# LoRA experts stage: masks made group by group, most router logits in the attention stage before, low-rank products one group ahead, and the B products as three rounded passes

## What is computed

```python
probs = softmax(x @ gate_w.T)                # 8 experts
vals, idx = top_k(probs, 2);  rw = vals / sum(vals)
common_w1 = x @ w_gate.T                     # shared by all experts, 256 -> 1024
common_w3 = x @ w_up.T
d1 = (x A1_e) B1_e * 2.0                     # rank 16 for each expert e
d3 = (x A3_e) B3_e * 2.0
act = silu(common_w1 + d1) * (common_w3 + d3)
out = (weight @ act) @ w_down.T + weight-sum of ((act A2_e) B2_e) * 2.0
```

## Time and profile before

| what | value |
|---|---|
| median of 3 runs | 2966.62 us (2965.15 to 2968.17) |
| the profiled execution: its own time | 2957.48 us |
| the profiled execution: its span | 2955.8 us |
| TensorE busy in the span | 2586.5 us (88%) |
| VectorE, ScalarE, GpSimd busy | 1778.2, 1340.0, 1104.7 us |
| the stage of the change, barrier to barrier | 898.1 to 1249.3 us |

### The profile page before, as it was taken

How to read it: one execution, slowest core, us unless ns; L and a number is a source line. 1 busy time by engine, 2 the same in 40 slices (tenths; PEclk the granted TensorE clock), 3 DMA queues, 4 the chain that set the end, 5 groups by cost and what they waited for, 6 DMA issues and landing times. The chain is left out here.

```text
span 2955.8 us, 56956 instructions
## 1 busy us (share of the span) xinstructions
PE 2586.5 (88%) x21304; PEld 2070.0 (70%) x21304; DVE 1778.2 (60%) x3911; ACT 1340.0 (45%) x2695; POOL 1104.7 (37%) x1396
## 2 busy tenths in 40 slices
PE   7999699997997999869699898888868994899995
PEld 7999477884875666536467666666745873899995
DVE  5665587125864333258488546787767874566665
ACT  4444366324673111147546533444433662465553
POOL 3444311003111222237612233643452112677773
PEclk9999799997998999979889999889977996899998
DMA  8887855327650000063276300000017743455663
GB/s 229 240 243 237 236 162 152 118 88 195 172 154 17 1 0 1 18 164 77 82 188 177 123 19 1 1 1 1 1 45 198 183 116 122 167 204 218 220 219 110
DMA packets 153626, 361.69 MB, mean 122 GB/s; under 512 B 26496, under 2 KB 110336, under 8 KB 138160
## 3 DMA queue, kind: packets, MB, share of 16 engines
q1 hardware_dynamic: 141632, 273.03, 32.8%
q0 software_dynamic: 11760, 85.51, 8.1%
HBM read 269.33 MB, written 88.67 MB: 121 GB/s over the span
## 5 line engine op out<-in xcount | busy, mean ns | idle before, releaser
L1210 ACT ACTIVATE arena<-ps 125x448 f32<-125x448 f32 x768 | 405.2, 545 | 328.2 <-PE ps L1118 324.5
L1244 DVE TENSOR_REDUCE arena<-ps 112x2 f32<-112x750 f32 x384 | 348.3, 930 | 84.2 <-PE ps L1102 81.2
L499 POOL TENSOR_SCALAR ln_var<-ln_mv 112x1 f32<-112x1 f32 x160 | 43.9, 275 | 759.1 <-DVE ln_mv L493 754.8
L1118 PEld LDWEIGHTS ps<-arena,wreg 98*125 98x125 bf16 x2304 | 215.9, 143 | 62.3 <-issue 19.2
L2925 PE MATMUL ps<-moe_x_r,moe_w_r 128*128 128x256 f32 x2016 | 255.0, 288 | 4.1 <-DVE arena L3085 2.7
L2925 PEld LDWEIGHTS ps<-moe_x_r,moe_w_r 128*128 128x128 f32 x2016 | 249.1, 194 | 7.2 <-DVE arena L3085 3.4
L1102 PE MATMUL ps<-wreg,arena 96*112 96x375 bf16 x768 | 216.9, 371 | 33.5 <-DMA arena<-query_parts 24.8
L1118 PE MATMUL ps<-arena,wreg 98*125 98x112 bf16 x2304 | 237.3, 228 | 4.8 <-ACT arena L1210 2.9
L1128 PE MATMUL ps<-arena 125*17 125x112 f32 x6144 | 199.1, 263 | 0.6 <-ACT arena L1210 0.6
L425 POOL TENSOR_TENSOR arena<-arena 128x375 bf16<-128x375 f32 x128 | 114.4, 917 | 169.9 <-ACT arena L362 169.9
L282 PE MATMUL ps<-kv_ctx_r,kv_w_r 128*128 128x376 f32 x768 | 146.2, 339 | 23.1 <-DVE kv_w_r L388 14.3
(11 more groups left out here) (353 smaller groups left out, 5847.8 us busy)
## 6 DMA issues: line engine op xcount, KB each, us to landing
wreg<-key_parts SPq DMA_DIRECT2D x288, 187.5 KB, 3.9
key_parts<-arena SPq DMA_DIRECT2D x128, 281.2 KB, 4.1
arena<-query_parts SPq DMA_DIRECT2D x108, 224.0 KB, 4.6
values<-arena SPq DMA_DIRECT2D x64, 357.0 KB
arena<-values SPq DMA_DIRECT2D x64, 357.0 KB
arena<-key_parts SPq DMA_DIRECT2D x96, 187.5 KB, 4.0
query_parts<-arena SPq DMA_DIRECT2D x40, 336.0 KB, 5.6
wreg<-in_e_w SPq DMA_DIRECT2D x16, 704.0 KB, 5.2
```

The lines of the kernel that those rows point to most:

```text
L1118: mm = pe.matmul(ps[0:KN, bank, g * T:(g + 1) * T], keys[r][:, hd, c * KN:(c + 1) * KN], queries(b)[:, hd, :], start=not masked, stop=not ...
L1210: act.activation(probs[k % PROBS], ps[0:KN, 4 + k % 2, 0:GT], ACT.Exp, scale=scale).then_inc(at_probs, 1)
L1244: dve.tensor_reduce(negmax[r % 2][:, 2 * p:2 * p + 2], ps[0:T, 2 * (p % 2):2 * (p % 2) + 2, 0:S2], AX.X, ALU.max, negate=True).then_inc(at ...
```

## The change

- **Logits.** 13 of the 16 sequences' router products move into the tail of `cross_stage`, 3, 3, 4 and 3 of them between the steps of its last chain; 3 stay at the head of the stage.
- **Head.** ScalarE makes the rounded half of x and of the weights, and of B1 and B3. GpSimd makes the other halves of x and of the gate and up weights, in a first part of 256 columns and a rest of 768; VectorE makes those of B. TensorE's order is: late logits, the low-rank products of group 0, the shared products of pieces 0 and 1, then the masks of group 0 alone.
- **Masks by groups.** The masks of group g + 1 are made inside group g, half at f = 3, half at f = 7. `weight_g` and the masks have two buffers.
- **B products.** The float32 product becomes three rounded ones, for which the masked low-rank values also need a rounded and a remainder part (`low_r`): 8 masking products a group where there were 4, and a difference of masks (`change`); VectorE makes 6 of the 8 and GpSimd 2, at the start of its `step(g)`.
- **One group ahead.** The low-rank products of group g + 1 run inside group g, behind the first quarter of the down products.
- A3 is loaded early, with the others.

```diff
+                if routed is not None:
+                    pe.wait_ge(early[1], routed.ready)
+                    pe.wait_ge(at_max, (n0 + B) * PAIRS)
+                logits(range(0, 3))
                 out.turn_back(pe, last, (B - 1) % 2)
+                logits(range(3, 6))
                 out.turn(pe, last, (B - 1) % 2)
+                logits(range(6, 10))
                 out.project(pe, last, (B - 1) % 2)
+                logits(range(10, B - LOGITS_LATE))
...
+            def masked_low(eng, g, part, q):
+                for k, m in ((0, mask_g[g % 2][:, 0, :]), (1, change)):
+                    eng.tensor_tensor(low_r[part][:, q, k, :], low[part][:, q, :], m, ALU.mult).then_inc(e1_lowm, 1)
+
             def gpsimd(pool):
                 top.make_ranks(pool)
+                pool.wait_ge(e1_weights, 1)
+                pool.tensor_tensor(x_r[1], xn_t[:, :, 0:GT], x_r[0].bitcast(F32), ALU.subtract).then_inc(e1_weights, 1)
+                for q in range(2):
+                    pool.wait_ge(e1_lowc, q + 1)
+                    split_w_low(pool, q, slice(0, FIRST)).then_inc(e1_wlow, 1)
+                for q in range(2):
+                    split_w_low(pool, q, slice(FIRST, F)).then_inc(e1_wlow, 1)
                 def step(g):
-                    pool.wait_ge(e1_weights, 3 * g + 3)
+                    pool.wait_ge(e1_low_lo, LOW_LO0 + 3 * (g + 1))
+                    pool.wait_ge(e1_maskc, 4 * (g + 1))
+                    masked_low(pool, g, 1, 0)
...
+                def hidden(f, k):
+                    for q in range(2):
+                        for n, (wp, xp) in enumerate(PRODUCTS):
+                            last = n == len(PRODUCTS) - 1
+                            mm = pe.matmul(ps[:, 2 + 2 * (f % 3) + q, 0:GT], b_r[wp][:, q, f * 128:(f + 1) * 128], low_r[xp][:, q, k, :],
+                                           start=False, stop=last, skip_group_check=k == 1)
+                    mm.then_inc(e1_hid, 1)
+                lows(0)
+                pe.wait_ge(e1_weights, 2)
+                pe.wait_ge(e1_wlow, W_LOW0 + 2)
+                for f in range(2):
+                    base(f)
+                for half in range(2):
+                    masks(0, half)
...
+                            if g > 0 or f >= 2:
+                                base(f)
+                            if f == 0:
+                                pe.wait_ge(e1_lowm, (g + 1) * 8)
+                            hidden(f, 0)
                         if f > 0:
                             pe.wait_ge(e1_act, g * (FC * 2) + when[f - 1, 0] + 1)
-                            hidden(g, f - 1, 1)
+                            hidden(f - 1, 1)
+                        if f in MASKS_AT and g < G - 1:
+                            masks(g + 1, MASKS_AT.index(f))
+                    if g < G - 1:
+                        pe.wait_ge(e1_maskc, 4 * (g + 2))
...
+                        if q == 1 and g < G - 1:
+                            lows(g + 1)
...
             def vector(dve):
+                for m in range(GB):
+                    widen(m)
+                low_low(0)
+                for m in range(GB, 2 * GB):
+                    widen(m)
+                for q in range(2):
+                    dve.wait_ge(e1_lowc, 2 + q + 1)
+                    dve.tensor_tensor(b_r[1][:, q], b_raw[:, q], b_r[0][:, q].bitcast(F32), ALU.subtract)
+                low_masked(0)
```

More of the change, by code:

```diff
@@ L1736, in make_ranks, with logits_pe @@
                     pool.memset(self.rank[:, :, e], float(E - e)).then_inc(const_made, 1)
-            def logits_pe(self, pe):
+            def logits_pe(self, pe, first=0):
                 pe.wait_ge(ln_evac, self.turned)
[L1740 to L1743, removed]
+                for b in range(first, B):
+                    mm = router_logits(pe, self.router, b)
                 mm.then_inc(rt_logits, 1)
@@ L1764, in choose @@
                 dve.wait_ge(rt_logits, self.n + 1)
[L1765 removed]
+                logits = ps[0:T, 0, LOGITS_AT:LOGITS_AT + B * E].rearrange("p (b e) -> p b e", e=E)
                 if self.bias is None:
@@ L1827, in lora_experts_stage @@
             wd, b2, router, a1, a2, w_raw = weights.wd, weights.b2, weights.router, weights.a1, weights.a2, weights.w_raw
-            wlow.take(128, (DC + FC) * ER)
-            a3 = arena.take(128, DC, ER)
-            b1, b3 = arena.take(128, F), arena.take(128, F)
+            a3 = weights.a3
+            wlow.take(128, (2 * DC + FC) * ER)
+            b_raw = arena.place(LORA_B_WORDS // 2, 128, 2, F)
+            arena.take(128, LORA_B_WORDS + LORA_LOW_WORDS)
+            b_r = [lora_b_r[:, part] for part in range(2)]
+            low_r = [lora_low_r[:, part] for part in range(2)]
             top = TopTwo(router)
@@ L1845, in lora_experts_stage @@
             scaled = [arena.take(128, GT) for _ in range(2)]
-            zm = [arena.take(128, GT) for _ in range(3)]
+            zm = [arena.take(128, GT), low[0][:, 0, :]]
             assert arena.at <= LORA_ACT
-            weights_ready = expect(3)
+            HALF = GB // 2 * T
+            weights_ready = expect(2)
             norm = RowNorm(x, **norm)
@@ L1880, in tensor @@
                 pe.wait_ge(early[1], weights.ready)
[L1881 to L1902, removed]
-                        mm = pe.matmul(dst, bq[:, f * 128:(f + 1) * 128], lowm[q][k], start=False, stop=True, skip_group_check=k == 1)
-                    mm.then_inc(e1_hid, 1)
@@ L1912, in step, with masks @@
                         mm.then_inc(e1_low, 1)
-                    at_least(pe, e1_added, g * GB)
-                    if g > 1:
-                        norm.evacuated(pe, (g - 1) * GB - 1)
-                    pe.wait_ge(e1_weights, 3 * g + 2)
-                    pe.wait_ge(e1_lowm, (g + 1) * 6)
+                def masks(g, half):
+                    bank = half_bank(g, half)
+                    if g == 0 and half == 1:
+                        pe.wait_ge(e1_low_lo, LOW_LO0 + 2)
+                    elif g > 0:
+                        pe.wait_ge(e1_maskc, 4 * g + 2 * half)
+                    for q in range(GB // 2):
+                        for k in range(2):
+                            m = (g * GB + half * (GB // 2) + q) * 2 + k
+                            cols = slice(k * HALF + q * T, k * HALF + (q + 1) * T)
+                            pe.wait_ge(e1_mask, m + 1)
+                            pe.matmul(ps[:, bank, cols], wide[m % MASKS].rearrange("p e r -> p (e r)"), ident16[:, :], start=True, stop=True)
+                            pe.transpose(ps[:, bank + 1, cols], wide_w[m % MASKS], ident[0:T, 0:T]).then_inc(e1_maskt, 1)
```

165 lines of the change are left out of this document (108 added, 57 removed).

## The result

The changed kernel takes **2937.61 us** at the median of 4 runs (2933.28 to 2938.67), the kernel before on the same chip 2965.89 us (4 runs, 2961.62 to 2968.17). The two medians are 28 us apart; the ratio is 0.9913, with a 95% interval of 0.9896 to 0.9929, which is 26 us less, between 21 and 31. The profiled execution took 2937.35 us, 20.1 less than the profiled one before, and its span is 2935.6 us.

A forecast was written before the change was run, and what follows sets the result against it. TensorE's time was taken to bound the groups, the longest chain the stage's head and the attention's tail. Terms 3.0 - 19.2 - 11.6 - 1.2 = -29 us gave 2928.5 us profiled, 2938 as median with 9 carried over; range 2928 to 2953.

The forecast's parts named there:

- Tail: End of the attention ahead of the stage: moved logits overrun the chain's holes; 3.0 us longer, between 2.1 and 3.75.
- Head: Stage start up to group 0's A2 products: first B product earlier, rounded products cheaper; 19.2 us shorter.
- All hidden: At the stage's start: GpSimd's remainders end before they are needed, the rests 13.6 us in, needed at 21.
- S+21 and S+60.3: Microseconds from stage start S: first B product at 21, group 0's first A2 product (z0) at 60.3.
- half-clock spell: Group 0's B products: 3.5 us at half clock after TensorE idles some 6 us; adds 1.7 us.
- Products: B products of groups 1 to 3: 3.5 us less in groups 1 and 2, 4.6 in group 3; 11.6 in all.
- boundaries: Steps between groups: TensorE waits 2.8 us for GpSimd's masking products; 5.8 against 6.2 us each, 1.2 less in all.
- The first: Stage start: GpSimd stands still during VectorE's two-tile operations and sets the length; gain 11 to 24 us; chance 0.2.
- its second case: Stage start: every GpSimd operation takes 3.3 instead of 1.29 us, queue 18 us late; gain 11, 2956 us; within chance 0.2.
- The second: Attention's end and group 0: logits hold the clock up, round trips are shorter; gain 33 to 37 us; chance 0.1.
- the third: TensorE's clock stays at 0.50 in group 0's products, A2 and down; slower, up to 30 us; chance 0.04.
- the fourth: Whole kernel: attention's end and new waits give back the gain; under 6 us, nothing measurable; chance 0.04.

The follow-up runs named there:

- the first trace: The changed kernel's first profiled execution, against the kernel before: 2937.35 us; median 2937.61 us, ratio 0.9913.
- the second: The changed kernel run and profiled once more, nothing edited: ratio 0.9912 to the kernel before.
- The float32 kernel: Changed kernel with its B products as one float32 product of the rounded parts, the two remainder products left out: ratio 0.9971 to the kernel before.

## Why the prediction was right, and where not

The median was forecast at 2938 and is 2937.6; the gain of 29 us lies in the measured 21 to 31. That the number came so close is luck. For the profiled execution the forecast was 2928.5 us, and it took 2937.35. The 9 us by which the old median lay above its profiled execution were carried over; the new median lies at its profiled execution, and the two errors cancel. The sum of the two places is 20.6 us less in the first trace and 24.4 in the second, where the forecast had 29; the stage alone is 24.1 and 28.5 us shorter, forecast 32. The first trace's 20.6 us are the whole difference of the two spans (20.2); the rest of the difference between the medians is not located, and it is within what the other stages shift by.

- **Tail, forecast +3.0:** +3.5 and +4.1. The mechanism is right (three sequences in 1.2 us at high clock, 2.1 at low); with logits back in the stage the tail is 9.3 us as before. The size moves with the moment at which the clock falls: the 16 loads ahead of `project` took 1.65 to 3.03 us in different executions, the tail of kernels with 13 sequences in it 12.8 to 15.1 us.
- **Head, forecast -19.2, measured -13.3.** This is the step that failed. "The choice starts at S+2.4 and needs 4.3 us": it started at S+2.55 and needed 12.1. "All hidden" of GpSimd's remainders was wrong in the other direction than the rival had it: GpSimd's own times were even below the forecast (a rest in 3.5 us instead of 3.9), and VectorE stood still behind them. The forecast let the choice wait 2.2 us for ScalarE's queue, and that hid a part of it: the exponential ran at S+14.6 instead of S+8.9, 5.7 us late. From there to the first B product it was 12.5 us, forecast 12.1, so it came at S+27.1, 6 us late, although masking products beside GpSimd's cost 1.7 us more (two at 1.45 instead of 0.6); the other steps of that stretch were shorter than forecast. With the rests on VectorE the forecast's S+21 and S+60.3 came out as 21.1 and 60.5, although the choice needed 6.1 us there and two masking products 1.45: the 2.2 us that the forecast had let it wait for ScalarE's queue took that in, and the exponential ran at S+8.6. The half-clock spell behind the first B product (1.7 us assumed) came: the clock was 0.50 up to 932 and 1.00 from 933, and from the first B product to z0 it was 39.4 us, forecast 39.3.
- **Products, forecast -11.6, and boundaries, -1.2:** together -10.7 in the first trace and -15.2 in the second. The float32 kernel confirms the price of the products. The new wait was there, with the forecast releaser; it was 2.0 instead of 2.8 us, for two reasons: GpSimd's masking product takes 1.03 us where 1.14 was taken, and the 12 shared products ahead of the wait took 2.8 us where 2.4 was taken. Four mask pairs in the loop took 0.6 us instead of 1.1. VectorE did release TensorE inside the f loop, which the prediction calls a sign of being wrong, but only at the stops that it had reckoned with: 0.9 us at the first k = 1, 0.62 at f = 8, 1.3 there in group 3. What the forecast lacked is that the clock falls behind the boundary wait in some places and not in others (1.6 us each time), and the products' pitch, 0.203 us in some stretches and 0.207 in others at a granted clock of 1.00, where 0.20 was taken (0.6 to 1.3 us a group); why it differs, I can't say.
- **Rivals.** The first had the right pair of engines, the right place and nearly the right price (a gain of 25 us), with the roles exchanged; its second case, GpSimd late by 18 us, did not occur. The second had the clock held up by the logits in the tail; it fell there all the same, to 0.50 at 895. The clock rose 3.4 us into group 0's products, so the third fell. The gain is clear of noise, so the fourth fell. The Trainium skill has the rule that decides the roles, in SBUF — State Buffer, section "SBUF: two separate sides": GpSimd and VectorE contend for a shared port pair that is locked for a whole instruction, and whichever starts first keeps it. The trace agrees, both ways round: 905.35 for GpSimd against 905.37 for VectorE, and VectorE waits to 906.78; at 924.14 VectorE's masking product starts first and keeps its 0.62 us, and GpSimd's, started at 924.18, takes 1.47 instead of 1.03. The prediction weighed only the general form of it and read the one row of 0.86 us, in which GpSimd was the late one, as a preference.

Not tried: logits back in the stage together with the rests on VectorE, so what the earlier logits gain in a head that GpSimd does not hold is open. The kernel with eight late logits bears on it: five sequences moved back cost the head 3.8 us and saved the tail 3.5.

## What to carry to other kernels

Work given to GpSimd "beside" VectorE is not hidden by GpSimd's having time: ask which VectorE operations with two SBUF inputs run in that stretch, and charge each with up to the whole of the GpSimd instruction that it meets. Long instructions of GpSimd belong where VectorE idles or where its work is not on the path; cutting them into pieces only spreads the same waits. And when a moved step leaves a queue's end as the last thing awaited, look one place up in that queue: two masking products placed ahead of two deviations took the whole 2-us wait away.

## What the runs showed of the hardware

- A VectorE operation of 0.29 us took up to 3.45 us beside a GpSimd instruction of 3.5 us, and a float32 copy with one input 1.18 instead of 0.17; the reductions of the choice (one input) took 0.29 us in every trace of the changed kernel and its variants. Of the two engines' loss VectorE bore nearly all (7.7 against 0.3 us).
- GpSimd's masking product of 448 columns takes 1.03 us alone and 1.41 to 1.47 beside VectorE's, VectorE's own 0.62 and 1.45: eight of them were done sooner by VectorE alone.
- After the same 2.0-us wait of TensorE the clock fell to 0.50 at one boundary (1.00 up to the wait's end, 0.66 over the 5 us behind it) and stayed at 1.00 at the next one of the same execution, and at all three of another.
